# Label adapter folded into the router and expert matrix per label, gathered per sequence, with the logits product in column tiles

## What is computed

```python
def cond2(x, label, W, lora_A, lora_B_w):          # label: one of 5 per sequence
    base  = einsum('bsi,oi->bso', x, W)
    low   = einsum('bsi,bir->bsr', x, lora_A[label])          # rank 32
    return base + einsum('bsr,or->bso', low, lora_B_w) * 0.5

def ffn(x, router_w, A, B):                        # 4 experts of rank 16, top 2
    logits = flat @ router_w.T
    gates  = softmax(top2(logits))
    mid    = einsum('tf,erf->ter', flat, A)
    return einsum('te,teo->to', gates, einsum('ter,eor->teo', mid, B) * 4)

x = x + attention(cond(x, slot, ...), Wq, Wk, Wv, Wo, cos, sin)   # 32 heads, 8 groups, causal
x = x + ffn(cond2(x, label, W, lora_A, lora_B_w), router_w, A, B)
```

## Time and profile before

| | |
|---|---|
| median of 3 runs | 213.74 us (213.51 to 214.06) |
| span of the profiled execution | 211.6 us (first to last instruction) |
| TensorE busy | 190.7 us, 90% of the span |
| VectorE busy | 136.3 us, 64% |
| ScalarE, GpSimd busy | 63.8 us, 63.0 us |
| one pass of the loop | 42.7 us |

### The profile page before, as it was taken

The page is one execution under the profiler, slowest core; times in us unless marked ns, Lnnn a source line. Parts: engine busy times, 40 slices in busy tenths (PEclk is TensorE's granted clock), DMA queues, the critical chain, the costliest instruction groups (busy, mean ns, idle before and its releaser), DMA issues.

```text
span 211.6 us, 3945 instructions
## 1 busy us (share of the span) xinstructions
PE 190.7 (90%) x1284; PEld 171.3 (81%) x1284; DVE 136.3 (64%) x313; ACT 63.8 (30%) x131; POOL 63.0 (30%) x81
## 2 busy tenths in 40 slices
PE   0899999979998999999999999999999998688862
PEld 0888999868977988999699989996999887576741
DVE  0395712389598936798786157997862579864363
ACT  2421301262253511332256102313461022632110
POOL 0422000198111118801111179011111674810000
PEclk9999959999999999999999999999999999999995
DMA  5937995243111100410141104101100041000202
GB/s 210 352 69 226 219 144 138 52 138 107 42 23 36 40 9 0 138 56 9 69 155 42 37 0 133 53 12 57 42 0 0 0 135 54 12 0 0 102 0 99
DMA packets 18619, 15.93 MB, mean 75 GB/s; under 512 B 7608, under 2 KB 12856, under 8 KB 18604
## 3 DMA queue, kind: packets, MB, share of 16 engines
q1 hardware_dynamic: 17164, 13.26, 23.8%
q10 hardware_dynamic: 1248, 2.29, 3.1%
q0 software_dynamic: 192, 0.20, 0.4%
HBM read 13.64 MB, written 2.10 MB: 74 GB/s over the span
## 4 chain that ended last, share of the span: by engine, by line
PE 75%; issue 7%; POOL 6%; DVE 5%; ACT 2%; DMA 2%; SPq 0%; POOLq 0%; DVEq 0%
PE bank L786 56%; PE bank L823 8%; PE bank L795 8%; PE bank L831 3%; POOL ex L448 2%; DMA xin<-x 2%; POOL Kbd L478 2%; POOL qr L470 1%; ACT PT L288 1%; DVE mx L550 1%; DVE sm L547 1%; DVE Vbd L596 1%; POOL A1l L443 1%; POOL sm L453 0%; DVE mg L653 0%
## 5 line engine op out<-in xcount | busy, mean ns | idle before, releaser
L448 POOL TENSOR_TENSOR ex<-ex,ri 128x512 f32<-128x512 f32 x16 | 16.8, 1050 | 56.2 <-DVE ri L562 56.2
L823 PE MATMUL bank<-xTh,WTh 128*128 128x256 f32 x64 | 18.7, 292 | 1.1 <-DVE WTl L714 1.1
L786 PE MATMUL bank<-yTh,Wqh 128*128 128x256 f32 x64 | 19.1, 298 | 0.3 <-DVE yTl L531 0.3
L786 PE MATMUL bank<-PT,Vbd 128*128 128x128 f32 x128 | 17.4, 279 | 2.0 <-ACT PT L288 2.0
L478 POOL TENSOR_TENSOR Kbd<-kr,K 128x256 f32<-128x256 f32 x32 | 18.7, 619 | 0.3
L786 PEld LDWEIGHTS bank<-PT,Vbd 128*128 128x128 f32 x128 | 15.6, 191 | 3.6 <-ACT PT L288 2.7
L786 PE MATMUL bank<-yTl,Wqh 128*128 128x256 f32 x64 | 18.4, 287 | 0.0
L786 PE MATMUL bank<-yTh,Wql 128*128 128x256 f32 x64 | 18.3, 285 | 0.0
L823 PE MATMUL bank<-xTh,WTl 128*128 128x256 f32 x64 | 17.8, 278 | 0.0
L823 PE MATMUL bank<-xTl,WTh 128*128 128x256 f32 x64 | 17.8, 278 | 0.0
L786 PE MATMUL bank<-Kbd,qr 128*128 128x256 f32 x64 | 17.0, 388 | 0.9 <-DVE sm L547 0.4
(11 more groups left out here) (134 smaller groups left out, 493.9 us busy)
## 6 DMA issues: line engine op xcount, KB each, us to landing
xin<-x SPq DMA_DIRECT2D x8, 256.0 KB, 2.9
xres<-x SPq DMA_DIRECT2D x8, 256.0 KB, 2.7
A2n<-L_cond_lora_A SPq DMA_DIRECT2D x32, 64.0 KB, 1.8
out<-x SPq DMA_DIRECT2D x6, 256.0 KB, 2.1
Wn<-L_cond_W ACTq DMA_DIRECT2D x4, 256.0 KB, 4.9
Wqn<-L_attn_Wq ACTq DMA_DIRECT2D x1, 1024.0 KB, 7.4
Wn<-L_cond_W SPq DMA_DIRECT2D x1, 1024.0 KB, 5.3
Wqn<-L_attn_Wo SPq DMA_DIRECT2D x8, 128.0 KB, 5.9
```

The source lines that it names most:

```text
L448: nc.gpsimd.tensor_tensor(ex[:, j], ex[:, j], ri[:, j, :, None].broadcast_to((P, 2 * NG, T)), ALU.mult).then_inc(normed, 1)
L786: return nc.tensor.matmul(dst, lhsT, rhs, start=start, stop=stop)
L823: nc.tensor.matmul(dst, w[u], z[r], start=(c % 2 == 0 and k == 0 and n == 0), stop=False, skip_group_check=True)
```

## The change

The label adapter is folded into the 68-column matrix, once per label: RL[label] = RT + lora_A[label] times C4. There are 5 labels, so RL has 5 x 68 columns for each of 4 slices of features. For each sequence, load_labels now fetches its 4 x 68 columns from RL (in SBUF) into RS, and mid_logits makes all of it in one step: for each tile, 4 slices times 4 sequences, each product with 32 stationary columns (the tokens of one sequence) and 68 moving columns, writing to 32 partitions of PSUM of its own (a column tile). label_in, label_mask and lay_labels are gone. In the prologue RT is computed transposed (RTT, 4 products of 512 columns), C4 is masked by VectorE into four parts, all five A matrices are loaded by one transfer, laid out by GpSimd and transposed on TensorE, and RL is made by three products for each of four slices, between v_spread(0, 1) and both(1, 0). SyncE waits for mid_ps where it waited for a2_laid. TensorE's loop over two passes is written out as a Python loop. Several of the new tiles lie in memory that is used later for others (x1T, PT, x1, xres).

```diff
@@ -99,8 +99,7 @@
         Wo = [sb(f"Wo{i}", [P, PH, D], F32R) for i in "hl"]
         Bw = sb("Bw", [P, KT, R2])
         RAT = sb("RAT", [P, KT, EW])
-        RT = sb("RT", [P, KT, EW])
-        C4 = sb("C4", [P, EW])
+        RL = sb("RL", [P, LABELS, KT, EW])
         BT = [sb("BTh", [P, D], F32R),
               sb("BTl", [E * R, D], F32R)]
         cs = sb("cs", [T, 2, HD])
@@ -144,9 +143,14 @@
         xres = sb("xres", [P, TT, D])
         x1 = sb("x1", [P, TT, D])
         x1T = sb("x1T", [P, TT, KT, P])
-        A2n = sb("A2n", [P, SEQ, KT, R2])
-        A2 = sb("A2", [P, KT, SEQ, R2])
-        lT = sb("lT", [P, TT, P])
+        RS = sb("RS", [P, SEQ, KT, EW])
+
+        A2T = x1T
+        RTT = PT[0:EW].rearrange("p j s h n -> p (j s h n)")[:, 0:D]
+        early = x1[:].rearrange("p t d -> p (t d)")
+        A2n = xres[:].rearrange("p t d -> p (t d)")[:, 0:LABELS * KT * R2].rearrange("p (l k r) -> p l k r", l=LABELS, k=KT)
+        A2 = early[:, 0:LABELS * KT * R2].rearrange("p (k l r) -> p k l r", l=LABELS, k=KT)
+        C4 = early[:, LABELS * KT * R2:][:, 0:4 * EW].rearrange("p (l n) -> p l n", l=4)
         mid = sb("mid", [P, TT, EW])
         m1 = sb("m1", [P, TT])
         lm = sb("lm", [P, TT, E])
...
@@ -218,8 +223,8 @@
             def load_labels(g):
                 for s in range(SEQ):
                     label = sp.value_load(ids[0:1, 1, bass.ds(g * SEQ + s, 1)], min_val=0, max_val=LABELS - 1)
-                    sp.dma_start(A2n[:, s].rearrange("p k r -> p (k r)"),
-                                 a2[bass.ds(label, 1)].rearrange("a (p k) r -> p (a k r)", k=KT)).then_inc(d_a2, 16)
+                    sp.dma_start(RS[:, s].rearrange("p k n -> p (k n)"),
+                                 RL[:, bass.ds(label, 1)].rearrange("p a k n -> p (a k n)")).then_inc(d_rs, 16)
 
             def load_xres(g):
                 for t in range(TT):
@@ -235,7 +240,7 @@
             def back_loads(g):
                 sp.wait_ge(x1_sb, TT * g)
                 load_xres(g)
-                sp.wait_ge(a2_laid, g)
+                sp.wait_ge(mid_ps, TT * g)
                 load_labels(g)
 
             def store(g):
@@ -260,11 +265,14 @@
             sp.dma_start(Bw[:], bw.rearrange("(c p) r -> p c r", p=P)).then_inc(d_bw, 16)
             sp.dma_start(Bf.rearrange("p e k r -> p e (k r)"),
                          fB.rearrange("e (p k) r -> p e (k r)", k=KT)).then_inc(d_bf, 16)
+            sp.dma_start(A2n, a2.rearrange("l (p k) r -> p l k r", k=KT)).then_inc(d_a2, 16)
             sp.wait_ge(wq_laid, KT)
             for g in range(NG):
                 sp.dma_start(Won[HD * g:HD * (g + 1)], wo.rearrange("(g h d) n -> g d h n", g=NG, h=PH)[g]).then_inc(d_o, 16)
             front_loads(1)
+            sp.wait_ge(a2_laid, 1)
             load_xres(0)
+            sp.wait_ge(RL_sb, KT)
             load_labels(0)
             with sp.Fori(0, G - 2) as g:
                 front_loads(g + 2)
@@ -294,12 +302,6 @@
                 else:
                     act.wait_ge(h_ps, g)
                 copy(A1[0][:].rearrange("p k s r -> p s k r"), A1n[:]).then_inc(a1_laid, 1)
-
-            def lay_labels(g):
-                act.wait_ge(d_a2, 16 * SEQ * (g + 1))
-                if not (isinstance(g, int) and g == 0):
-                    act.wait_ge(low_ps, TT * g)
-                copy(A2[:].rearrange("p k s r -> p s k r"), A2n[:]).then_inc(a2_laid, 1)
 
             def x_cols(g):
                 for h in range(2):
@@ -371,7 +373,6 @@
                 ctx_copy(b, 1)
                 exp(b, 3)
                 pt_copy(b, 2)
-                lay_labels(b)
                 q_cols(a, 1)
                 ctx_copy(b, 2)
                 pt_copy(b, 3)
@@ -393,16 +394,20 @@
             act.wait_ge(d_b, 16)
             y_cols(0, 0)
             y_cols(0, 1)
-            act.wait_ge(RT_ps, 1)
-            copy(RT[:].rearrange("p c n -> p (c n)"), PTB[:, 0:KT * EW]).then_inc(RT_sb, 1)
+            act.wait_ge(RTT_ps, 1)
+            copy(RTT, PTB[0:EW]).then_inc(RTT_sb, 1)
             q_cols(0, 0)
             q_cols(0, 1)
             kv_cols(0)
-            act.wait_ge(C4_ps, 1)
-            copy(C4[:], OUT[:, 0:EW]).then_inc(C4_sb, 1)
             act.wait_ge(BT_ps, 1)
             nc.scalar.mul(BT[0][:].rearrange("q (p k) -> q k p", k=KT),
                           CTX[:].rearrange("q (k p) -> q k p", k=KT), 4.0).then_inc(BT_h, 1)
+            for n, src in enumerate((PTB, OUT)):
+                act.wait_ge(A2T_ps, n + 1)
+                copy(A2T[:, n].rearrange("p k n -> p (k n)"), src[:]).then_inc(A2T_sb, 1)
+            for k in range(KT):
+                act.wait_ge(RL_ps, k + 1)
+                copy(RL[:, :, k], [PTB, OUT][k % 2][:, 0:LABELS * EW].rearrange("p (l n) -> p l n", l=LABELS)).then_inc(RL_sb, 1)
             act.wait_ge(d_o, 16 * NG)
             for h in range(PH):
                 copy(Wo[0][:, h], Won[:, h]).then_inc(Wo_h, 1)
...
@@ -490,6 +494,8 @@
             pool.wait_ge(d_ids, 32)
             load_slots(pool, 0, range(POOL_SLOTS), d_slot_pool)
             adapters_rest(0)
+            pool.wait_ge(d_a2, 16)
+            nc.gpsimd.tensor_copy(A2.rearrange("p k l r -> p l k r"), A2n).then_inc(a2_laid, 1)
             pool.wait_ge(CS_sb, 1)
             k_times_cos(0)
             rope(0)
@@ -605,11 +611,6 @@
                 if not (isinstance(g, int) and g in (0, G - 1)):
                     dve.wait_ge(d_out, 16 * TT * g)
                 V.tensor_tensor((dst or x1)[:, t], tb[t][:], xres[:, t], ALU.add).then_inc(x1_sb, 1)
-
-            def label_mask(g, t, tb=TB):
-                dve.wait_ge(low_ps, TT * g + t + 1)
-                V.tensor_tensor(lT[:, t].rearrange("p (s t) -> p s t", t=T), tb[t][:, 0:P].rearrange("p (s t) -> p s t", t=T),
-                                K[:, C_LABEL:C_LABEL + 4, None].broadcast_to((P, 4, T)), ALU.mult).then_inc(low_sb, 1)
 
             def gates(g, one=None, tb=TB):
 
@@ -702,9 +703,7 @@
                 q_times_sin(a, 1)
                 residual(b, 1)
                 v_blocks(a, 0)
-                label_mask(b, 0)
                 v_blocks(a, 1)
-                label_mask(b, 1)
                 shift(a, 0)
 
             V.memset(gr[:], 0.0).then_inc(zeroed, 1)
@@ -737,6 +736,9 @@
             dve.wait_ge(d_bw, 16)
             V.tensor_copy(Bw4, Bw[:, :, None, :].broadcast_to((P, KT, 4, R2))).then_inc(bw_laid, 1)
             dve.wait_ge(d_bf, 16)
+            dve.wait_ge(C4_ps, 1)
+            V.tensor_tensor(C4, OUT[:, None, 0:EW].broadcast_to((P, 4, EW)),
+                            K[:, C_LABEL:C_LABEL + 4, None].broadcast_to((P, 4, EW)), ALU.mult).then_inc(C4_sb, 1)
             for i in range(2):
                 V.tensor_copy(Bk[:, :, i].rearrange("p k (e r) -> p k e r", e=E), Bf.rearrange("p e k r -> p k e r")).then_inc(bf_laid, 1)
             q_split(0, 0)
@@ -770,10 +772,8 @@
             ctx_rest(b, 3, SMALL)
             mgT_rest(b - 1)
             finish(b - 1)
-            label_mask(b, 0, LB)
             residual(b, 1, LB, xres)
             gates(b, 0, LB)
-            label_mask(b, 1, LB)
             mgT_rest(b, 0, LB)
             gates(b, 1, LB)
             mgT_rest(b, 1, LB)
@@ -927,18 +927,14 @@
                     i = tr(tb[t][:, P * k:P * (k + 1)], (src or x1)[:, t, k:D:KT])
                 i.then_inc(x1T_ps, 1)
 
-            def label_in(g, t, tb=TB):
+            def mid_logits(g, t, tb=TB):
                 pe.wait_ge(x1T_sb, TT * g + t + 1)
-                pe.wait_ge(a2_laid, g + 1)
+                pe.wait_ge(d_rs, 16 * SEQ * (g + 1))
                 for k in range(KT):
-                    i = mm(tb[t][:, 0:P], A2[:, k, 4 * t:4 * t + 4].rearrange("p s r -> p (s r)"), x1T[:, t, k], k == 0, k == KT - 1)
-                i.then_inc(low_ps, 1)
-
-            def mid_logits(g, t, tb=TB):
-                pe.wait_ge(low_sb, TT * g + t + 1)
-                for k in range(KT):
-                    mm(tb[t][:, 0:EW], x1T[:, t, k], RT[:, k], k == 0, False)
-                mm(tb[t][:, 0:EW], lT[:, t], C4[:], False, True).then_inc(mid_ps, 1)
+                    for s in range(4):
+                        i = mm(tb[t][T * s:T * (s + 1), 0:EW], x1T[:, t, k, T * s:T * (s + 1)], RS[:, 4 * t + s, k],
+                               k == 0, k == KT - 1)
+                i.then_inc(mid_ps, 1)
 
             def mid_transpose(g, t, tb=TB):
                 pe.wait_ge(g_mid, 2 * (TT * g + t + 1))
@@ -1000,10 +996,8 @@
                 x1_transposes(b, 0)
                 v_spread(a, 0)
                 x1_transposes(b, 1)
-                label_in(b, 0)
                 scores(a, 0)
                 v_spread(a, 1)
-                label_in(b, 1)
                 scores(a, 1)
 
             pe.wait_ge(d_K, 16)
@@ -1032,10 +1026,9 @@
             i.then_inc(CS_ps, 1)
             pe.wait_ge(RAT_sb, 1)
             pe.wait_ge(d_w2, 16)
-            for k in range(KT):
-                for c in range(KT):
```

(31 more changed lines are left out.)

8 lines of the change are left out of this document (4 added, 4 removed).

## The result

The changed kernel is **slower**: the ratio to the kernel before is 1.027, 95% interval 1.0245 to 1.0289; the median of its four executions is 221.82 us (219.51 to 226.35) against 213.7. The profiled one is the 219.81 us with 0.967.

What follows compares the result with a forecast made beforehand. TensorE, busy 90% of the 211.6 us span, was taken as the bound. Prologue +7.7, hand-overs -1.0, tail -0.2 and clock +1.0 sum to +7.5 on 213.74: 221.2 us, range 217.8 to 225.0.

Steps and rivals of the forecast that it cites:

- RTT: Prologue, TensorE: 4 products with 512 moving columns replace 16 of RT, 3.4 us, 4.1 less, with no clock fall.
- VectorE holds the gain back: Prologue: VectorE's wait for C4 delays q_split and v_rest, which ends at 40.0; TensorE idles 4 us before rotation of k.
- Clock fall in the prologue, +1.0: Prologue, after TensorE's idle time from 36.0 to 40.0: lower clock halves rotation and spread of V, +1.0 us.
- RL block: Prologue, before both(1, 0): making RL takes 1.4 us for each of four k, ending at 52.7 on ScalarE.
- Who waits behind it: Prologue: Wo copies, lay_adapters and x_cols queue behind ScalarE's RL copies, so y_base(1, 0) starts at 57.3, +7.7 us.
- Column tile: mid_logits: only neighbouring products overlap, 1.5 us a tile of tokens, plus 0.4 per stretch for changing the array's shape.
- Hand-over: Where one loop pass meets the next: -0.5 us each, at most -0.83 because VectorE's x_rest decides; two give -1.0.
- rival (a): mid_logits: column tiles run one after another at 1.9 us, hand-overs 2 x 0.4; +10.4, 224.1 us; chance 0.22.
- rival (d): Tiles overlap fully at 0.5 us and VectorE's chain moves up with TensorE: -1.1, 212.6 us; chance 0.03.
- Tail: From the third hand-over on: label_in goes, the last two mid_logits cost more; -0.2 us, bounds -1.6 to +0.8.
- rival (b): Column tiles overlap well at 1.1 us and the clock holds: +4.9, 218.6 us; chance 0.20.
- Moved transfers: A matrices land near 31, POOL's 640-column copy takes 1.7 us, label transfers land in up to 4 us: no cost.

Runs made afterwards that it cites:

- e2: Changed kernel, but VectorE masks C4 after the first block-diagonal V, not ahead of the q splits: 216.72 us, ratio 1.0135 to the kernel before.
- c1: Changed kernel with 28 unused products on TensorE in the idle time before the rotation of k: 220.27 us, ratio 1.0322 to the kernel before.
- e1: Changed kernel, but ScalarE makes the four Wo copies ahead of the A2T and RL copies: 220.61 us, ratio 1.0341 to the kernel before.
- g1: Changed kernel, but in mid_logits four products in a row go to the same column tile: 219.62 us, ratio 1.0259 to the kernel before.
- k1: Changed kernel with 14 unused products on TensorE in the idle time before adapter_in: 219.72 us, ratio 1.0248 to the kernel before.
- k2: Changed kernel with C4 masked later, Wo copies right after kv_cols, and 14 unused products before adapter_in: 212.63 us, ratio 0.9937 to the kernel before.
- e6: Changed kernel with C4 masked after the first block-diagonal V and Wo copies right after kv_cols: 214.42 us, ratio 1.0013 to the kernel before.

## Why the prediction was right, and where its sizes were off

The forecast was 221.2 us (217.8 to 225.0), slower at 0.92. Measured: 221.82 as the median, 219.81 in the profiled execution; both inside the range, and the cause is the one forecast. Step by step:

- **RTT**: 3.4 us forecast, 3.62 measured with the length of the last, 512 moving columns at 0.43 a record, and no fall of the clock. Right.
- **VectorE holds the gain back**: v_rest was to end at 40.0, it ended at 40.09; TensorE idle 4 us, measured 3.83. Right, and e2 shows it is this wait.
- **Clock fall in the prologue, +1.0**: it fell at 40.0 and stayed down until 43.4. From the rotation of k to y_base(1, 0) the change takes 17.99 us (40.24 to 58.23) and e2, without the fall, 16.78 (36.73 to 53.51): 1.2 less. Right in size; e2 and c1 show that the idle time causes it.
- **RL block**: 1.4 us for each k; the RL copies of ScalarE start 1.37 apart (49.21, 50.58, 51.96, 53.34). The last ended at 53.8, forecast 52.7 + 1.0 for the clock.
- **Who waits behind it**: y_base(1, 0) forecast at 57.3 + 1.0 = 58.3, measured 58.23. Right. But this step taken by itself is not a price that moving the Wo copies gives back, as e1 shows.
- **Column tile**: mis-sized. 1.5 us a tile of tokens forecast, and about 0.2 in and out for the change of mode. Measured: 64 records in 0.93 us from the first start to the last, so 0.47 a tile of tokens, the lower bound of the prediction ("if four column tiles overlap wholly"). The four tiles' records start 6.6 ns apart, and the next four 0.059 us after the first of these, about the distance that the RAT transposes with 68 columns had. The sentence that failed is "only neighbours can overlap", which no row had shown: all four tiles ran at once. Even one tile after another costs only about 1.2 us (g1), not 1.9. The loads are shorter too: 0.106 to 0.110 us with 32 stationary columns, where those with 128 columns of x1T were 0.186 to 0.203 before.
- **Hand-over**: -0.5 each forecast, -0.83 as the most. Measured -0.72, and -0.7 in the next pass without the clock's part, since the cheap tiles take TensorE off this path. (At 1.9 us a tile the prediction's own terms give +0.3, not the +0.4 of rival (a).) That VectorE's chain up to x_rest would decide was right, and the reason why rival (d), 212.6 us, did not come: the 1.9 us that TensorE is ahead turn into idle time.
- **What was missing**: that this new idle time lets the clock fall as well. I had a fall in the prologue only. In the profiled execution it cost 1.5 us at the second hand-over, which turned -0.7 into +0.80; k1 and k2 show that the fall goes when the idle time is filled. The median (+8.1) stands above the profile's +6.5 because of two of the four executions, which had lower mean granted clocks, 0.946 and 0.930; where in them the clock fell is not on record.
- **Tail**: -0.2 forecast, -2.3 measured. The working of the tail with 0.5 us in place of 1.5, with its change of mode kept, gives -0.9 - 0.9 - 2 x 0.16 - 0.1 = -2.2: the same mis-sized term. In the rows, the stretch from the third hand-over to x1_transposes(b, 0) (199.40) is 0.9 shorter than before, the one from there to mid_logits(b, 0) (205.48), where label_in stood, 0.8, and the one to the last transpose of mg (212.25) 0.7. The prediction's lower bound, -1.6 at 1.1 us, is a slip: the same terms give -1.1, as in rival (b).
- **Moved transfers**: the A matrices had landed when GpSimd's copy of them began at 29.84, forecast near 31. POOL's copy of 640 columns took 0.72 us, not 1.7. The label transfers are now 136 KB and land in 2.0 us, not 4. All hidden, as forecast.

With tiles at 0.5 us, and hand-overs and tail as they then come out, the sum would have been +7.7 + 1.0 - 1.4 - 2.2 = +5.1, 218.8; the fall at the hand-over, 1.5, was missing and brings it to 220.3, near the profiled 219.81. So part of the closeness of 221.2 is luck, two errors against each other: tiles too dear by 2.4 us in all, and a clock fall not counted. Rival (b), with tiles at 1.1 us, had the hand-overs and the tail nearer; what it had wrong is that the clock holds.

The Trainium skill (TensorEngine Tiling (Array Packing), Key Properties) says that different tiles load and multiply in parallel; the trace agrees (starts 6.6 ns apart, and 1.16 us where g1's order takes 2.53). Its figure that I drew an estimate of 0.8 us a tile from (TensorE: Matmul & The Clock Gate, Packing small matmuls) is for another shape; here 0.5 was measured.

**Open.** Which idle time brings a fall in which execution is not settled: the 2.2 us before y_base were followed by none in the profiled execution of the change and by one in c1 and in k1. Nor is idle time the only cause: before the change the clock fell at 25.7 us, inside the R^T products, where TensorE had no gap but its records were 0.234 us apart. And the mean granted clock alone does not give the time: one execution of e6 took 213.93 us with 0.928. A place for the RL block beside other work was not tried.

## What to carry to other kernels

Price a saving at the engine that is late next: here TensorE's work shrank by several microseconds at three places, and at each it was VectorE or ScalarE that kept its time. Before you put a wait into an engine's program, read what is queued behind it, and who waits for that; a wait for C4 in front of seven operations that did not need it left TensorE idle for 3.83 us, where the products it waited for take 1.0. Where several parts are changed together, try each alone: the one that moved the wide operand, read contiguously at 512 columns, was worth 2.5% by itself, while the whole change with three repairs (C4 late, the Wo copies moved, the gap filled) is worth 0.6%. In no kernel measured here did the folding save more than it cost.
